# A constant row of the output projection: from a sum on Pool in the first stage to a one-row product on PE in cross attention

## The reference, cut to what matters

```python
x = x + self_attention(layernorm(x))                  # one head, causal
x = x + cross_attention(layernorm(x), ctx, mask)      # 16 heads of 8 channels
x = x + ffn(layernorm(x))                             # quantised, 384 hidden
# inside cross_attention, at its end:
x = einsum('bhqk,bhkd->bhqd', p_attn, v) ...          # heads put side by side
return x @ Wo.T + bo                                  # with v = value @ Wv.T + bv
```

## Time and profile before

| | us |
|---|---|
| median of 3 runs | 374.4 |
| the three runs | 376.76, 369.46, 374.4 |
| the profiled execution | 369.51 |
| its span | 367.7 |
| first stage, to the first `pv` | 0 to 102 |
| cross attention | 102 to 234 |
| feed-forward network | 234 to 368 |

### The profile page before, as it was taken

One profiled execution on the slowest core, in us unless ns is written; L12 is line 12 of the kernel. 1 busy time (PEld: TensorE's weight loads), 2 busy tenths in 40 slices (PEclk: granted clock), 3 DMA queues, 4 the chain that ended last, 5 costly groups with the idle time before them and its releaser, 6 DMA issues.

```text
span 367.7 us, 9555 instructions
## 1 busy us (share of the span) xinstructions
PE 308.6 (84%) x3621; PEld 204.2 (56%) x3621; DVE 282.1 (77%) x589; ACT 248.0 (67%) x452; POOL 177.7 (48%) x321
## 2 busy tenths in 40 slices
PE   3999999997599998989889899689987668660996
PEld 2697877774366665656556566434432223220996
DVE  5369988876767878888887885858779967897563
ACT  3368888875358787778778776268697736991850
POOL 3559999973313474755666471100058841662000
PEclk9999999999759999999999999889998998895699
DMA  5961666665640000000000000000000000000034
GB/s 139 299 193 32 200 206 205 200 206 160 213 133 2 5 2 4 4 3 4 2 4 4 4 4 2 0 0 0 2 0 1 0 0 0 1 0 0 18 98 116
DMA packets 23751, 22.67 MB, mean 62 GB/s; under 512 B 3545, under 2 KB 21402, under 8 KB 23578
## 3 DMA queue, kind: packets, MB, share of 16 engines
q1 hardware_dynamic: 22170, 21.78, 19.5%
q10 hardware_dynamic: 1536, 0.28, 0.4%
HBM read 15.75 MB, written 6.31 MB: 60 GB/s over the span
## 4 chain that ended last, share of the span: by engine, by line
PE 41%; DVE 22%; POOL 17%; issue 8%; ACT 7%; DMA 2%; SPq 1%; ACTq 1%; POOLq 0%; DVEq 0%
DVE mxs L1537 8%; PE banks L834 7%; PE banks L655 7%; PE banks L874 7%; PE banks L616 4%; DVE nm L1331 4%; POOL rstd L352 3%; PE banks L677 3%; POOL X L448 3%; POOL pickd L371 2%; PE banks L673 2%; PE banks L668 2%; PE banks L621 2%; DMA k_dram<-klo 2%; PE banks L536 2%
## 5 line engine op out<-in xcount | busy, mean ns | idle before, releaser
L1331 DVE TENSOR_REDUCE nm<-banks 128x8 f32<-128x1024 f32 x64 | 78.0, 1219 | 21.7 <-PE banks L612 21.7
L1028 ACT ACTIVATE PT<-banks,bmask,vmask 128x1024 f32<-128x1024 f32 x64 | 76.8, 1200 | 2.1 <-PE banks L621 2.1
L834 PE MATMUL banks<-X3T,upT 128*128 128x512 f32 x96 | 48.9, 660 | 15.4 <-DVE mxs L1537 9.4
L484 POOL TENSOR_TENSOR G<-ng,sq 128x1536 int32<-128x1536 int32 (+3 forms) x9 | 26.1, 2903 | 43.6 <-DVE sq L1562 43.6
L1537 DVE TENSOR_REDUCE mxs<-G 128x1 f32<-128x1536 int32 (+4 forms) x27 | 41.9, 1566 | 6.7 <-ACT G L1064 6.7
L655 PE MATMUL banks<-PT,VP 128*32 128x128 f32 x1024 | 43.0, 287 | 0.4
L834 PEld LDWEIGHTS banks<-X3T,upT 128*128 128x128 f32 x96 | 19.1, 208 | 43.4 <-issue 20.6
L908 ACT ACTIVATE h<-X,shift,rstd 128x128 f32<-128x128 f32 x64 | 26.4, 482 | 13.9 <-POOL shift L397 13.8
L655 PEld LDWEIGHTS banks<-PT,VP 128*32 128x32 f32 x1024 | 25.7, 112 | 8.1 <-issue 0.7
L1016 ACT ACTIVATE oT<-banks 128x128 f32<-128x128 f32 x32 | 8.9, 277 | 30.9 <-PE banks L673 30.9
L433 POOL CAST NM<-nm 128x64 bf16<-128x64 f32 x32 | 7.6, 238 | 43.8 <-DVE nm L1331 43.8
(11 more groups left out here) (183 smaller groups left out, 710.8 us busy)
## 6 DMA issues: line engine op xcount, KB each, us to landing
kd<-k_dram SPq DMA_DIRECT2D x32, 128.0 KB, 2.7
qd<-q_dram SPq DMA_DIRECT2D x32, 128.0 KB, 2.5
ctxg<-in_ctx_dram SPq DMA_DIRECT2D x8, 256.0 KB, 3.2
X3T<-m_dram SPq DMA_DIRECT2D x1, 1792.0 KB, 10.1
out_dram<-y SPq DMA_DIRECT2D x7, 256.0 KB, 2.3
X<-in_x_dram SPq DMA_DIRECT2D x3, 512.0 KB, 10.0
k_dram<-khi SPq DMA_DIRECT2D x8, 128.0 KB, 1.8
k_dram<-klo SPq DMA_DIRECT2D x8, 128.0 KB, 2.2
```

Of the source, the lines that this page charges most:

```text
L834: m = pe.matmul(bank(2 + FC * (g % 2) + k), w[:, k * P:k * P + P], grp(X3T, g), start=True, stop=True)
L1028: act.activation(PT[:, a, :], bank(2 + 2 * a, 2), ACT.Exp, bias=bmask[:, n:n + 1], scale=vmask[:, n:n + 1]).then_inc(S["t_exp"], 1)
L1331: V.tensor_reduce(nm[:, n % 2, 2 * NSET * a:2 * NSET * (a + 1)], bank(0, 2).rearrange("p (h m) -> p h m", m=P), AX.X, ALU.max, negate=True ...
```

## The change

The sum on Pool is removed. `project(n)` now starts its accumulation with a product of one row: `ones[0:1, :]` (one partition, 128 columns) against `cbias[0:1, :]`, in fp32, and the projection is added to it. And `project(n - 1)` moves from before `both(n, 1)` to behind it.

```diff
-            def add_constant(g):
-                if g == 0:
-                    pool.wait_ge(S["w_cbc"], 1)
-                pool.wait_ge(S["l_h"], GB * g + GB)
-                xg = grp(X, g).rearrange("p (b d) -> p b d", d=P)
-                nc.gpsimd.tensor_tensor(xg, xg, bc(cbias[:, :].unsqueeze(1), [P, GB, P]), ALU.add).then_inc(S["l_cb"], 1)
...
-                if live(i - 3):
-                    add_constant(i - 3)
...
             def project(n):
                 pe.wait_ge(S["t_oTc"], n + 1)
-                pe.matmul(bank(6 + n % 2)[:, P:2 * P], oT[:, :], WXT[:, 3, :], start=True, stop=True).then_inc(S["t_wo"], 1)
+                pe.matmul(bank(6 + n % 2)[:, P:2 * P], ones[0:1, :], cbias[0:1, :], start=True, stop=False)
+                pe.matmul(bank(6 + n % 2)[:, P:2 * P], oT[:, :], WXT[:, 3, :], start=False, stop=True).then_inc(S["t_wo"], 1)
...
                 pe.wait_ge(S["t_exp"], 2 * n + 2)
                 pv(n, 1)
+                both(n, 1)
                 if n > 0:
                     project(n - 1)
-                both(n, 1)
                 if B - TAIL <= n < B - 1:
                     turn_early_rows3(n)
```

More of the change, by code:

```diff
@@ L205, in decoder @@
             s_pow s_stat s_agg s_var s_neg s_rstd s_h s_hT s_hTc s_a s_ac s_v s_vc s_s s_nm s_exp s_pT s_pTc s_pv s_inv s_x1
-            l_pow l_stat l_agg l_var l_neg l_rstd l_h l_hT l_hTc ld_mr0 ld_mr l_pd l_pe l_pick l_cT l_cTc l_k l_khi l_klo l_q l_qhi l_qlo l_v l_vc l_cb l_qst l_kst
+            l_pow l_stat l_agg l_var l_neg l_rstd l_h l_hT l_hTc ld_mr0 ld_mr l_pd l_pe l_pick l_cT l_cTc l_k l_khi l_klo l_q l_qhi l_qlo l_v l_vc l_qst l_kst
             t_k0 t_k1 t_q0 t_q1
```

## The result

The changed kernel takes 381.98 us in the median of four runs, against 372.86 us for the kernel before: a ratio of 1.0335 with a 95% interval of 1.0275 to 1.0395, so it is slower. The profiled execution takes 382.67 us, with a span of 380.9; that of before took 369.51, with 367.7. In the changed kernel lines behind 376 have moved up by 8 to 10: `turn` is L663, `project` L667 (the one-row product) and L668 (the projection), the copy of it on ACT L1013, DVE's reduction L1322.

A forecast was written before the change was run, and what follows sets the result against it. Pool, with PE close behind, bounded the first stage; a chain through ACT, PE and DVE bounded the cross attention. There +22.2 us, less 2.0 in the first stage, gave +20.2 on 372.5: 392.7 us, range 382 to 401.

The forecast's parts named there:

- the cheapest case of the sum: Whole kernel: one-row product at 0.22 us, +15.1 us on the profiled execution, giving 384.6 us.
- a shorter `both`: Cross attention on PE: allowance for `both` taking less time, putting the range a little under 384.6 us.
- The start of `both(n, 1)` at 1.13 us: Cross attention on PE: begins 1.13 us after the turn instead of 1.25, waiting for DVE's reduction; gain 0.12 us.
- part 3: Cross attention, `project` behind `both(n, 1)`: one-row product costs 0.42 us (bounds 0.22, 0.50); `project` ends at 2.59, not 1.32.
- The iterations with `largest3`: Five cross attention iterations of 4.66 us: DVE's chain at 4.54, PE's 4.68 binds, adding 0.1 us together.
- The iteration of 4.07: One cross attention iteration, forecast to grow by 0.6 us.
- the early one of 4.20: One iteration at the start of the cross attention, forecast to grow by 0.5 us.
- The end of the cross attention: Last iterations and bare last `project`: more PE time ahead of the transposes, +1.3 us, bounds 0 and 2.
- The first stage: Pool's sum removed: PE limits steps at 8.7 us, gain -2.0 us, bounds -4.9 and 0.
- The rival that gave Pool's full 4.9 us: First stage: Pool the only real limit, giving back 4.9 us; part of (b), chance 0.04.
- (a): Cross attention: copy doesn't bind, iterations grow 0.2 us by PE's work; about +2 us, 374 to 376; chance 0.13.
- (b): Both stages: Pool gives back 4.9 us, `project` disappears under ACT's exp; 367 to 369 us; chance 0.04.

The follow-up runs named there:

- the 128-row product: The changed kernel with the one-row product made 128 rows, all ones against the constant row divided by 128: 384.0 us, ratio 1.0407 to the kernel before.
- the run with the order alone: The kernel before with only `project(n - 1)` moved behind `both(n, 1)`, Pool's sum kept, no one-row product: 380.54 us, ratio 1.0305.

## Why the prediction was right, and where its size was off

*Direction and mechanism* were right: slower, because `pv(n, 0)` waits for ACT's copy of a projection that now ends last. The size was too large by half, +20.2 us against +13.2 between the profiled executions. The forecast of 392.7 us was besides added to 372.5, while the kernel before took 369.1 in the median of the 13 executions beside the later runs. 381.98 was measured, which is the lowest edge of the range (382 to 401) and 2.6 us under the cheapest case of the sum (384.6). That the range reaches down to the result is luck: it was stretched there for a shorter `both`, and `both` kept its length. The start of `both(n, 1)` at 1.13 us came out exactly (157.29), with DVE's reduction as its cause; so did the distance of 1.72 from `pv(n, 0)` to the next turn, and the end of `both` at 1.68 (the 128-row product's first load).

*The term that was mis-sized* is the price of the one-row product in part 3, taken as 0.42 with bounds 0.22 and 0.50. It was 0.10, under the lower bound. The 0.42 is right for the product itself, which took 0.41 or 0.42 from its first load to the next one's in all three places. What part 3 had wrong is the overlap: it let the product start only when `both(n, 1)` had ended, at 1.68, and it started at 1.37, its two weight loads in among those of the injected maxima. The comparison with 128 rows, which don't slip in there, gives 0.22. Besides, PE resumed 0.11 us behind the copy instead of 0.05; that could have been read from the kernel before, where `pv(n, 0)` starts 0.11 us behind the copy's end (166.00 to 166.11). So the iteration grew by 0.68 and not by 0.94: over 21 iterations 14.3 us instead of 19.7. With 0.10 the prediction's own sum is 2.27 for the end of `project`, and 4.36 for the iteration; with 0.11 for the way back as well it is the measured 4.42.

*The iterations with `largest3`* were said to be bound by DVE at 4.54 or by PE at 4.68; with the smaller price DVE's 4.54 stood, and five of them gained 0.12 each. The iteration of 4.07 became 4.42 (+0.35, where 0.6 was forecast), the early one of 4.20 became 4.43.

*The end of the cross attention*: +1.3 was forecast, about +0.5 measured (13.6 us over the last three iterations instead of 13.7, and 0.6 more behind the last turn, which is no more than that stretch varies between traces). The prediction counts 30 iterations and there are 31: the last, of 4.62 us, is missing from its list, and it is 4.62 in the changed kernel too. For the last sequences `both(n, 1)` has no reduction to wait for and starts at once, which I had not taken into account.

*The first stage*: -2.0 forecast, -1.75 at the first turn (-1.8 at the first `pv` in the run with the sum alone gone), with PE as the limit at 8.57 us a step. The length of a step is sure; what the whole stage gained is known only to about 1 us. The rival that gave Pool's full 4.9 us was wrong.

*The sum*: +20.2 forecast, +13.2 between the profiled executions, +12.4 by the ratio. The rivals (a), PE's work alone, and (b), faster, both had the projection's end not binding; the run with the order alone refutes them. What (a) describes is real in another place: in the old order the one-row product costs 0.34 us an iteration of PE's time.

*The rule on row groups* (the Trainium skill, TensorE: Matmul & The Clock Gate, Part 3, "The mechanism": a weight load overlaps matmuls in flight only when its row group differs) fits the one-row product better than I used it. The injected maxima of `both(n, 1)` are at rows 64 to 127, the one row at row 0, and its loads were served between theirs; the projection, which shares row 0 with it, loaded only 0.41 us behind its first load. It doesn't fit the 128-row product: all its rows are shared with the projection, and the projection's load came after 0.22 us. So the rule alone doesn't give the size.

## What to carry to other kernels

Before an instruction is moved behind a block of work, ask who waits for its result, and when: a projection that PE could do in a gap of its own cost 0.6 us an iteration once it stood right ahead of the point at which PE waits for the copy of that projection. The time at which the consumer is ready (here 1.63 us after the turn) is the deadline, and in these traces everything later, from 1.98 to 2.40, was paid one to one. For small work look for an engine that waits anyway, at a place with slack on both sides: the sum that held up the first stage was free on Pool one stage later, and cost time at each of the three places on PE that were tried.

## What the runs showed of the hardware that I had not expected

The price of the same one-row product depended on its neighbours: 0.42 us in the old order, 0.10 us behind a stream of products in tiles of 32 rows. The time from its first load to the next one's hardly changed (0.42 and 0.41); what changed is that 0.31 us of it ran beside that stream. There the weight load of the product, which comes after all eight of L611 in the program, was served in their midst (157.53, between 157.47 and 157.58).

How long two passes of 128 columns held up the next load went, in the rows that I compared, by what came next. That load came 0.41 or 0.42 us behind the first load where it has another number of rows (from 1 to 128: 157.53 to 157.94 in the changed kernel; from 128 to 32: 164.92 to 165.34 in the kernel before), and 0.22 us behind it where it has the same number (128 and 128: 157.93 to 158.15 with 128 rows). Why is not shown.
